# AdaLN block with a test-time-training attention and a routed expert layer: eight expert blocks taken beside the last attention chunk

## The reference, cut to what matters

```python
h = layernorm(x) * (1 + ca) + sa
x = x + ga * attn(h)
h = layernorm(x) * (1 + cb) + sb
x = x + gb * ffn(h)

# attn: q, k, v and three learning rates from h; 16 chunks of 128 rows here (b*l), 4 heads of 128
def step(carry, inp):                       # one chunk
    gate = ki @ w0_;  hb = ki @ w2_;  sg = silu(gate);  hidden = sg * hb
    dhidden = vi @ w1_.transpose(0, 2, 1)
    ...
    w1g = newtonschulz5(einsum('bch,bcd->bhd', hidden * lr1i, vi))      # 2 steps, also w0g, w2g
    w1_ = w1_ + w1g                                                      # also w0_, w2_
    w0_ = w0_ / (norm(w0_, axis=1) + 1e-05) * w0n                        # also w1_, w2_
    oi = silu(qi @ w0_) * (qi @ w2_) @ w1_
# then an RMS norm per head and W_proj

# ffn: 8 experts, top 2 of a softmax router (with a low-rank part)
gup = einsum('th,eho->teo', xf, gate_up_proj) + SCALING * low_rank
gates, h = split(gup, 2);  h = silu(gates) * h
out = einsum('tei,eih->teh', h, down_proj) + SCALING * low_rank
y = the two selected experts' rows, weighted and added
```

## Time and profile before

| what | value |
|---|---|
| median of 3 runs (lowest, highest) | 979.37 us (974.23, 980.03) |
| the profiled execution's own time | 979.38 us |
| its span, first to last instruction | 977.7 us |
| TensorE busy | 874.9 us (89%) |
| VectorE, ScalarE, GpSimd busy | 661.5, 647.9, 349.9 us |
| mean granted TensorE clock | 0.957 |
| moved by DMA | 120.43 MB |

### The profile page before, as it was taken

The page is one execution under the profiler, slowest core; times in us unless marked ns, Lnnn a source line. Parts: engine busy times, 40 slices in busy tenths (PEclk is TensorE's granted clock), DMA queues, the critical chain, the costliest instruction groups (busy, mean ns, idle before and its releaser), DMA issues.

```text
span 977.7 us, 16358 instructions
## 1 busy us (share of the span) xinstructions
PE 874.9 (89%) x5127; PEld 534.0 (55%) x5127; DVE 661.5 (68%) x2299; ACT 647.9 (66%) x1416; POOL 349.9 (36%) x285
## 2 busy tenths in 40 slices
PE   7888998999989989899898999997638999999995
PEld 3556566565665756656566575664414444444442
DVE  3687989889898898988989888876541222222221
ACT  2767888888888898888988888876303343333431
POOL 2223444453443534445344453432311222232222
PEclk8999999999999999999999999988658999999998
DMA  9755326164261542615426233157433455444530
GB/s 332 268 152 163 100 97 174 39 179 106 91 195 40 157 109 87 196 49 147 124 73 195 64 101 98 55 160 325 154 149 76 81 93 92 91 83 78 96 61 0
DMA packets 59092, 120.43 MB, mean 123 GB/s; under 512 B 6896, under 2 KB 8560, under 8 KB 57984
## 3 DMA queue, kind: packets, MB, share of 16 engines
q1 hardware_dynamic: 50688, 102.28, 34.9%
q0 software_dynamic: 8176, 16.85, 9.3%
q10 hardware_dynamic: 144, 0.26, 0.1%
HBM read 51.94 MB, written 69.27 MB: 124 GB/s over the span
## 4 chain that ended last, share of the span: by engine, by line
PE 59%; DMA 14%; DVE 12%; POOL 5%; ACT 5%; issue 4%; SPq 1%; POOLq 0%; ACTq 0%
PE bank L712 14%; DMA xs_scratch<-t_arena 12%; PE bank L110 10%; PE bank L116 8%; PE bank L729 7%; POOL xs_scratch L1816 2%; PE bank L549 1%; PE bank L559 1%; PE bank L487 1%; PE bank L467 1%; PE bank L568 1%; PE bank L503 1%; PE bank L543 1%; PE bank L498 1%; PE bank L480 1%
## 5 line engine op out<-in xcount | busy, mean ns | idle before, releaser
L110 PEld LDWEIGHTS bank<-t_arena 128*128 128x128 bf16 (+1 forms) x1536 | 123.4, 122 | 82.9 <-issue 15.4
L110 PE MATMUL bank<-t_arena 128*128 128x128 bf16 (+1 forms) x1536 | 152.3, 236 | 8.6 <-DVE t_arena L862 2.3
L712 PE MATMUL bank<-t_arena 128*128 x312 | 143.0, 601 | 2.4 <-ACT t_arena L1731 2.4
L116 PE MATMUL bank<-t_ident,t_arena 128*128 128x128 f32 x618 | 102.8, 286 | 41.6 <-DMA t_arena<-xs_scratch 8.4
L116 PEld LDWEIGHTS bank<-t_ident,t_arena 128*128 128x128 f32 x618 | 72.8, 144 | 98.9 <-issue 40.4
L1842 POOL DMA_INDIRECT out_x<-t_arena,t_tokx x39 | 60.6, 1553 | 183.1 <-DVE t_small L1369 173.0
L1724 ACT ACTIVATE t_arena<-bank 128x256 f32<-128x256 f32 x39 | 15.0, 384 | 123.3 <-PE bank L712 123.3
L1374 DVE TENSOR_TENSOR t_arena<-t_arena,bank 128x256 f32<-128x256 f32 x39 | 16.4, 421 | 118.3 <-ACT t_arena L1724 118.3
L712 PEld LDWEIGHTS bank<-t_arena 128*128 128x128 f32 x312 | 57.0, 192 | 60.4 <-issue 60.4
L729 PE MATMUL bank<-t_arena 128*128 x156 | 73.5, 593 | 0.5 <-ACT t_arena L1719 0.5
L1731 ACT ACTIVATE t_arena<-bank,t_small 128x128 f32<-128x128 f32 x156 | 58.6, 455 | 15.7 <-PE bank L116 13.6
(11 more groups left out here) (510 smaller groups left out, 2190.7 us busy)
## 6 DMA issues: line engine op xcount, KB each, us to landing
xs_scratch<-t_arena SPq DMA_DIRECT2D x16, 2064.0 KB, 12.1
wm_scratch<-t_arena SPq DMA_DIRECT2D x48, 256.0 KB
t_arena<-wm_scratch SPq DMA_DIRECT2D x8, 1536.0 KB, 12.6
t_arena<-xs_scratch SPq DMA_DIRECT2D x39, 258.0 KB, 2.7
t_arena<-in_gate_up SPq DMA_DIRECT2D x32, 256.0 KB, 3.8
t_arena<-in_wmod SPq DMA_DIRECT2D x6, 1024.0 KB, 11.3
t_arena<-in_down SPq DMA_DIRECT2D x16, 256.0 KB, 3.7
out_x<-t_arena SPq DMA_DIRECT2D x16, 256.0 KB, 2.0
```

Of the source, the lines that this page charges most:

```text
L110: mm = pe.matmul(bank[:, s], lhs[:, s], rhs[:, s], start=True, stop=True)
L116: mm = pe.transpose(bank[:, 128 * k:128 * k + 128], src[:, 128 * k:128 * k + 128], idn)
L712: mm = pe.matmul(AA[u % 2][:, :], xT[u % 2][:, 128 * k:128 * k + 128], w_e[:, bass.ds(which[u], 1), 512 * k:512 * k + 512], start=(k == 0) ...
```

## The change

Eight of the 39 blocks (EB = 8) are taken out of the tail. They are full blocks of 128 rows, chosen from the counts of chunks 0 to 13: a first table (TA) rounds each expert's count down to whole blocks and takes the first eight. The last round of the chunk loop (chunk 15, with the apply of chunk 14), the last apply and the eight blocks are now one written stretch on each engine. The second table covers what is left, NF = 31 blocks. So that all expert weights can be loaded as the last chunk begins, the low-rank updates run one chunk ahead (chunk 0 does two sets), and the tiles in SBUF are laid out anew. `units()` has new groups: sets 0 to 14 each lie in three row groups, set 15 in two. RING is 6, `yb` is gone (the weighted rows go back into `xg`), `ft` is gone (silu writes `fs`). The early blocks share one up bank (P1) and one bank (P2) for their transpose and down product.

```diff
-NB = 2 * NC + NE - 1
-RING = 4
+EB = 8
+NF = 2 * NC + NE - 1 - EB
+NB = EB + NF
+RING = 6
...
+    without = (3, 2, 1, 0, 3, 2, 1, 0, 3, 2, 1, 0, 3, 2, 3)
+    out = [[left[q].pop(0) for q in range(4) if q != without[m]] for m in range(NC - 1)]
+    return out + [left[2] + left[3]]
...
+        def AA(u):
+            return P1 if u < EB else [A0, A1][u % 2]
+        def BB(b):
+            return P2 if b < EB else [B2, P2][b % 2]
+        def CC(b):
+            return P2 if b < EB else B0
```

```diff
-            for c in range(NC):
+            for c in range(NC - 1):
...
+                if c == 0:
+                    for j, (e, k) in enumerate(UNITS[0]):
+                        mm = pe.matmul([P0, P1, P2][j][:, :], la[e % 2][q, 128 * k:128 * k + 128], lb[k // 4][q, :], start=True, stop=True)
+                    mm.then_inc(mgf_pe, 1)
+                if c == 0:
+                    pe.wait_ge(mgf_dve, nth(MGF_DVE, 0, "u2"))
+                if c >= 1:
+                    pe.wait_ge(mg_dve, nth(MG_DVE, c-1, "u2"))
+                for j, (e, k) in enumerate(UNITS[c + 1]):
...
+            pe.wait_ge(apply_dve, nth(APPLY_DVE, NC - 3, "pe"))
+            heads(pe, A0, W[0], qT[0]).then_inc(apply_pe, 1)
+            pe.wait_ge(apply_dve, nth(APPLY_DVE, NC - 3, "cum"))
+            pe.matmul(P0[:, 0:8], onesb[:, :], cum[(NC - 2) % 2][:, :], start=True, stop=True).then_inc(ta_pe, 1)
+            heads(pe, B2, kT[1], W[2]).then_inc(fwd_pe, 1)
+            heads(pe, B0, kT[1], W[0]).then_inc(fwd_pe, 1)
...
+            pe.wait_ge(n2_act, nth(N2_ACT, NC - 1, "XT0"))
+            heads(pe, B2, NXT[2], NXT[2]).then_inc(n2_pe, 1)
+            pe.wait_ge(s_g[0], 16)
+            turned(pe, P0, xg[0 % RING], 4, ident[:, :]).then_inc(tn_pe, 1)
...
+            heads(pe, B0, NX[0], NTT[0]).then_inc(n0_pe, 1)
+            pe.wait_ge(s_e, 128)
+            for k in range(4):
+                mm = pe.matmul(AA(0)[:, :], xT[0][:, 128 * k:128 * k + 128],
+                               w_e[:, bass.ds(which[0], 1), 512 * k:512 * k + 512], start=(k == 0), stop=(k == 3))
+            mm.then_inc(up_pe, 1)
```

```diff
+            dve.wait_ge(n1_dve, nth(N1_DVE, NC - 1, "nsr"))
+            dve.tensor_tensor(h4(NX[1]), h4(XH[1]), bc(nsr[1]), ALU.mult).then_inc(n1_dve, 1)
+            dve.wait_ge(s_g[0], 16)
+            dve.tensor_scalar(tokx[0 % RING], xg[0 % RING][:, 512:513].bitcast(U32), 2047, None, ALU.bitwise_and).then_inc(tn_dve, 1)
+            dve.wait_ge(n0_pool, nth(N0_POOL, NC - 1, "nb1"))
+            dve.tensor_scalar(nb2[0], nb1[0], 2e-07, None, ALU.add).then_inc(n0_dve, 1)
...
+            dve.tensor_tensor(h4(NX[2]), h4(XH[2]), bc(nsr[2]), ALU.mult).then_inc(n2_dve, 1)
...
+            dve.tensor_tensor(h4(NX[0]), h4(XH[0]), bc(nsr[0]), ALU.mult).then_inc(n0_dve, 1)
```

SyncE, behind the loop over chunks 0 to 14:

```diff
+            sp.wait_ge(prep_pe, len(PREP_PE) * NC)
+            sp.wait_ge(s_ms, 48 * (NC - 1))
+            for n in range(2):
+                sp.wait_ge(s_z[n], 8 * NC)
+            expert(0)
+            expert(1)
+            expert(4)
+            sp.wait_ge(mg_dve, nth(MG_DVE, NC - 2, MG_DVE[-1]))
+            store_tiles(NC - 1)
...
+            expert(2)
...
+            expert(3)
+            sp.wait_ge(s_ms, 48 * NC)
+            sp.wait_ge(s_o[0], 16 * (NC // 4))
             for e in range(5, NE):
                 expert(e)
+            sp.wait_ge(s_sc, 448)
+            sp.wait_ge(ta_dve, nth(TA_DVE, 0, "row"))
...
+            at = sp.value_load(row0u[0:1, 0:0 + 1], min_val=0, max_val=2048 * NE - 128)
+            sp.dma_start(xg[0 % RING], xs[bass.ds(at, 128), :]).then_inc(s_g[0 % RING], 16)
...
+            sp.wait_ge(s_sa, 16)
+            at = sp.value_load(row0u[0:1, 6:6 + 1], min_val=0, max_val=2048 * NE - 128)
+            sp.dma_start(xg[6 % RING], xs[bass.ds(at, 128), :]).then_inc(s_g[6 % RING], 16)
```

More of the change, by code:

```diff
@@ L241, in adaln_block @@
         wx = [sm(1) for _ in range(RING)]
-        cnt, nblk, ends, st0, dV, V9 = sm(NE), sm(NE), sm(NE), sm(NE), sm(NE), sm(NE + 1)
+        full, ends, step8, done, rem, last = [sm(NE) for _ in range(6)]
+        nu = sm(NE).bitcast(U32)
         s_c, s_lr, s_blr, s_wproj, s_onw, s_gA, s_gB, s_gw, s_lora, s_sc, s_ms, s_e, s_sa = [
@@ new lines, in _ @@
+            heads(pe, A0, W[0], qT[1]).then_inc(apply_pe, 1)
+            pe.wait_ge(n2_act, nth(N2_ACT, NC - 1, "W"))
+            heads(pe, A1, W[2], qT[1]).then_inc(apply_pe, 1)
+            pe.wait_ge(dn_act, nth(DN_ACT, 1, "fT"))
+            for k in range(2):
+                mm = pe.matmul(BB(1)[:, :], fT[1][:, 128 * k:128 * k + 128],
+                               w_e[:, bass.ds(which[1], 1), 2048 + 512 * k:2560 + 512 * k], start=(k == 0), stop=(k == 1))
+            mm.then_inc(dn_pe, 1)
@@ new lines, in _ @@
+            mm.then_inc(dn_pe, 1)
+            pe.wait_ge(tn_act, nth(TN_ACT, 6, "xT"))
+            for k in range(4):
+                mm = pe.matmul(AA(6)[:, :], xT[0][:, 128 * k:128 * k + 128],
+                               w_e[:, bass.ds(which[6], 1), 512 * k:512 * k + 512], start=(k == 0), stop=(k == 3))
+            mm.then_inc(up_pe, 1)
+            pe.wait_ge(s_g[1], 32)
+            turned(pe, P0, xg[7 % RING], 4, ident[:, :]).then_inc(tn_pe, 1)
+            pe.wait_ge(up_dve, nth(UP_DVE, 6, "fs"))
@@ new lines, in _ @@
+            pe.wait_ge(dn_dve, nth(DN_DVE, 5, "y"))
+            turned(pe, CC(6), fs[0], 2, ident[:, :]).then_inc(dn_pe, 1)
+            pe.wait_ge(dn_act, nth(DN_ACT, 6, "fT"))
+            for k in range(2):
+                mm = pe.matmul(BB(6)[:, :], fT[0][:, 128 * k:128 * k + 128],
+                               w_e[:, bass.ds(which[6], 1), 2048 + 512 * k:2560 + 512 * k], start=(k == 0), stop=(k == 1))
+            mm.then_inc(dn_pe, 1)
+            pe.wait_ge(tn_act, nth(TN_ACT, 7, "xT"))
@@ L1349, in _ @@
[L1349 to L1354 removed]
+            dve.tensor_tensor(last, ends, full, ALU.subtract).then_inc(tab_dve, 1)
+            dve.wait_ge(tab_dve, nth(TAB_DVE, 0, "v0"))
```

1285 lines of the change are left out of this document (1016 added, 269 removed).

## The result

The changed kernel takes 968.58 us (median of 4 runs, 965.46 to 970.02) where the kernel before took 979.7 beside it: ratio 0.9896, 95% interval 0.9871 to 0.992. It is faster by a little over 1%; the prediction was 962.4, with a range from 945 to 977. The profiled execution took 967.92 us, its span 966.2.

What follows compares the result with a forecast made beforehand. TensorE bounds the expert blocks, latency the last chunk and apply. Naive gain 46.5 us, mostly given back (14.5 gather wait, 2.2 early table, rest slower blocks), leaves 17: 979.4 - 17 = 962.4 us; range 945 to 977.

Steps and rivals of the forecast that it cites:

- the mark: Start of block 8's up matmul, behind which all work is unchanged: 767 instead of 784.03 us, -17 us.
- Part 1: Low-rank updates one chunk ahead: chunk 0 costs +4 us, chunks 12 to 14 save 4.2; together 0 us.
- Part 2: Early table: chunk 15's forward heads stand behind the count over 14 chunks on TensorE; +2.2 us (bounds 0 and 5).
- Part 3: Expert loads: first gather queues behind them at 425 GB/s, lands at 683.5 us; VectorE waits 14.5 us.
- rival 1: Gathers do not queue behind the experts, or loads run faster: wait about 1 us, 948 us in all; chance 0.18.
- Part 4: From 683.5 us to the last weight transpose: pieces of 15 and 19 us, ending at 717.5 (bounds 711, 724).
- Part 5: Last apply to its rank matmul: early blocks' work fits the chain's waits, 26 us (23 to 32), rank at 743.5.
- Part 6: Blocks 5 to 7, behind the rank matmul: 7.1 us each, 21.3, then 2.1 more; block 8's up matmul at 767.
- Rival 2: Interleaving costs more: parts 4 and 5 at their upper bounds (+6.5, +6), 974 to 977 us; chance 0.16.
- Rival 3: Expert stream slow, about 210 GB/s: 13.4 MB take 64 us, first gather lands at 714, 993 us; chance 0.07.

Runs made afterwards that it cites:

- e5: Kernel before with only the new assignment of low-rank units to chunks: 971.9 us, ratio 0.9935.
- e8: e7 with the forward heads of chunk 15 ahead of the early table's count matmul and the heads of chunk 14's apply on TensorE: 952.7 us.
- e1: Changed kernel with the six early gathers issued on SyncE ahead of the loads of experts 5 to 7: 958.2 us.
- e6: Changed kernel with the six early gathers issued from ScalarE's DMA queue instead of SyncE's: 962.7 us.
- e7: Changed kernel with expert loads begun early, gathers ahead of experts 5 to 7, chunk 0's second low-rank set behind its weight transposes: 952.4 us.
- e10: Changed kernel with only the old assignment of low-rank units to sets put back: 971.3 us, ratio 0.9947.

## Why the prediction was right, and where it was off

The direction, the mechanism and the place were right, the gain was 11.7 us at the mark instead of 17. By the prediction's own steps, in the profiled execution:

- **Part 1**, forecast 0. The doubled set costs 4.7 us net of a clock that is higher for the heads behind it (7.05 later at the heads, less 1.1 that was there before the sets, less 1.25 for 2.17 instead of 3.42 us), forecast 4. By the start of the last set 2.9 are given back, and 1.3 more in chunk 14. At chunk 14's rank matmul (654.33) the changed kernel is 1.65 us behind, 1.1 of it from the first 77 us. Right. What I had not seen is that the half that saves doesn't need the half that costs: the assignment alone gives 4 to 6 us (e5).
- **Part 2**, forecast 2.2: the heads of chunk 15 start 3.9 us after those of before, less 1.65: 2.3. Right, and worth nothing here, since the wait for the gather covers it (e8).
- **Part 3** is the step that failed, by size. The mechanism is shown by e1 and e6, and rival 1 falls. But the loads began at 652.1 and not 649, since the clear was issued at 640.57 (+3, the delay from chunk 0 that I had set to nothing), and the stream ran at 373 GB/s beside the stores and the scatter of chunk 13 and only afterwards at 416 to 426, where I had taken 425 for all of it. The first landing was at 689.99, so that the forecast of 683.5 was 6.5 us too early. VectorE's wait was 19.3 us, forecast 14.5. Two of the prediction's own signs were missed by this: 400 GB/s or more from 649 us on, and a wait of 12 to 16 us.
- **Part 4**, from the landing to the last weight transpose: 33.1 us (690.0 to 723.1), forecast 34. That the sum is right is in part luck. Up to block 0's up matmul it took 17.8 us, forecast 15, and from there 15.3, forecast 19, of which 3.4 were for that matmul at half clock:

```profile
707.79 3.65 PE L802 MATMUL bank<-t_arena 128*128 x8
```

  It ran at full clock: the granted clock was 0.50 up to 696 us, then 0.93, 0.61 from 700 to 704, and 1.00 from 704 on.
- **Part 5**, to the rank matmul: 24.7 us (747.85), forecast 26.
- **Part 6**: 24.5 us, forecast 23.4. Blocks 5 to 7 start 7.4 and 7.3 us apart, forecast 7.1:

```profile
747.95 3.69 PE L913 MATMUL bank<-t_arena 128*128 x8
755.37 3.60 PE L930 MATMUL bank<-t_arena 128*128 x8
762.70 3.60 PE L945 MATMUL bank<-t_arena 128*128 x8
```

Of the 5.3 us by which the mark was missed, then, the landing has 6.5, and parts 4 to 6 came out 1.1 us better than forecast. The whole time was missed by 6.2 us (968.6 and 962.4), by 5.5 in the profiled execution (967.92). Rival 2 (the interleaving costs more) was wrong: the eight blocks slipped in at the forecast price, within the errors of part 4 that cancel. Rival 3 (a slow stream) was the direction of the miss, at 373 GB/s and not 210.

## What to carry to other kernels

When a transfer is moved behind large ones on its queue, ask two things: how many bytes stand ahead of it, and what stands behind the instruction that first waits for it; here changing the order of issue alone gave 9 to 10 us (9.4 in S) and moving only the waiting instructions 5 to 7 (6.6 in S), with not a byte less. Once one such wait is gone, expect the next one (the experts, then the clock) within a few us: five further edits, each aimed at 1 to 7 us, moved the time together by 9. And where a change joins several edits, time the smallest one alone: a reassignment of units that costs nothing gave about half the gain.

## What was not expected of the hardware

- Two hardware queues share the DMA engines by packets, not by bytes (328 and 325 packets in 10 us, 3.63 and 0.60 MB). Here a short-row transfer on a queue of its own got 60 GB/s beside a long-row one at 363.
- Rows of 2 KB moved more slowly than rows of 12 KB even alone. In e7, from 670 to 676 us, with hardly anything but gathers in flight, 728 packets carried 1.42 MB, 236 GB/s at a DMA share of 0.84; in the changed kernel from 674 to 686 the experts' 465 packets carried 5.11 MB, 426 GB/s at a share of 1. The 236 GB/s is also set by the issue, since 0.264 MB every 1.1 to 1.5 us is 180 to 240 GB/s. What the rows themselves cost is told by the busy time alone: by an estimate from these figures 236 / 0.84 = 280 GB/s while busy.
- What the clock does in a short stretch can outweigh a saving there. In the profile before the clock fell to 0.50 in chunk 14's set (3.22 us) and stayed there for the 2.82 us of transposes; in e5, with a set of 1.13 us, it stayed at 1.00. With the old units in the changed kernel (e10) the fall is seen earlier, at 568 us, in a set that took 3.20 us. It is one profile each, and the same stretch came out either way in kernels with the same code there, so that the shorter set kept the clock up is not shown. Why the clock fell in these places and not elsewhere no run tells.
